# Second attention of a four-layer kernel: another instruction order on each engine, the second normalization on ScalarE, and the weights of two attentions asked for a stage earlier

## The reference

```python
def fake_quant(x, s, qn, qp):                       # round to a step of s, clipped
    xc = jnp.clip(x / s, qn, qp)
    xr = xc + jax.lax.stop_gradient(jnp.round(xc) - xc)
    return s * xr
qkv = jnp.einsum('bnc,dc->bnd', x, Wqkv)...         # x: normed tokens
q = fake_quant(q, s_q, -4, 3) * scale
k = fake_quant(k, s_k, -4, 3)
v = fake_quant(v, s_v, -4, 3)
attn = jnp.einsum('bhnd,bhmd->bhnm', q, k)
attn = fake_quant(attn / N, s_attn, 0, 7)
out = jnp.einsum('bhnm,bhmd->bhnd', attn, v)
out = fake_quant(out, s_after, -4, 3)
return out @ Wproj.T + bproj
```

## Time and profile before

| what | value |
|---|---|
| time, median of 3 runs | 2672.78 us |
| the profiled execution's own time | 2677.54 us |
| its span | 2675.4 us, 52026 instructions |
| granted TensorE clock, mean | 0.907 of full speed |
| PE busy | 2346.2 us, 88% |
| DVE busy | 1339.4 us, 50% |
| ACT busy | 852.6 us, 32% |
| POOL busy | 493.8 us, 18% |
| second attention | 615.6 to 876.8 us of the span |
| third attention, start | 1253.2 us |

### The profile page before, as it was taken

The page is one execution under the profiler, slowest core; times in us unless marked ns, Lnnn a source line. Parts: engine busy times, 40 slices in busy tenths (PEclk is TensorE's granted clock), DMA queues, the critical chain, the costliest instruction groups (busy, mean ns, idle before and its releaser), DMA issues. The chain is left out here.

```text
span 2675.4 us, 52026 instructions
## 1 busy us (share of the span) xinstructions
PE 2346.2 (88%) x17821; PEld 2039.7 (76%) x17821; DVE 1339.4 (50%) x3887; ACT 852.6 (32%) x2082; POOL 493.8 (18%) x583
## 2 busy tenths in 40 slices
PE   6968999995998489997999766999978899999997
PEld 5967999993666389986788655778747788888886
DVE  1665333333786711112688743555566446372744
ACT  0421222222555033332232212343444343343421
POOL 0214322221332334443122101000011000010100
PEclk8978999995787699998999856999989999999999
DMA  4103545512110267673000001000000452726355
GB/s 105 26 23 113 180 139 169 178 46 54 33 34 16 81 198 243 213 228 104 18 18 9 1 1 28 8 7 9 7 12 26 142 146 66 205 54 174 90 150 156
DMA packets 241583, 234.74 MB, mean 88 GB/s; under 512 B 29624, under 2 KB 223022, under 8 KB 241326
## 3 DMA queue, kind: packets, MB, share of 16 engines
q1 hardware_dynamic: 226798, 203.52, 26.8%
q0 software_dynamic: 11520, 27.54, 3.1%
q10 hardware_dynamic: 3136, 2.03, 0.3%
HBM read 277.77 MB, written 35.45 MB: 117 GB/s over the span
## 5 line engine op out<-in xcount | busy, mean ns | idle before, releaser
L740 PE MATMUL f_pg<-f_vxT,f_w 128*128 128x128 f32 x2112 | 261.2, 278 | 3.0 <-DVE f_vxT L810 3.0
L740 PEld LDWEIGHTS f_pg<-f_vxT,f_w 128*128 128x128 f32 x2112 | 251.8, 194 | 7.9 <-DVE f_vxT L810 4.4
L752 PE MATMUL f_po<-f_wd,f_hid 128*128 128x192 f32 x1440 | 254.3, 326 | 1.2 <-DVE f_vout L836 0.7
L752 PEld LDWEIGHTS f_po<-f_wd,f_hid 128*128 128x128 f32 x1440 | 231.2, 190 | 2.0 <-issue 1.7
L713 POOL DMA_INDIRECT f_answers<-f_vout,f_to_row x120 | 118.5, 987 | 418.6 <-DVE f_vout L834 250.7
L821 DVE TENSOR_TENSOR f_hid<-f_silu,f_pg 128x128 f32<-128x128 f32 x336 | 81.5, 283 | 218.8 <-ACT f_silu L789 204.0
L789 ACT ACTIVATE f_silu<-f_pg 128x128 f32<-128x128 f32 x336 | 78.2, 276 | 292.9 <-PE f_pg L746 275.2
L794 ACT ACTIVATE f_hid<-f_pg,f_b 128x128 f32<-128x128 f32 x384 | 111.2, 368 | 186.8 <-issue 102.2
L810 DVE COPY f_vxT<-f_pt 128x256 f32<-128x256 f32 x120 | 50.5, 421 | 208.5 <-PE f_pt L732 208.5
L746 PE MATMUL f_pg<-f_vxT,f_wr 64*128 64x128 f32 x2112 | 150.9, 284 | 0.0
L1900 DVE TENSOR_REDUCE a_low<-a_s_bank 96x6 f32<-96x1152 f32 x64 | 86.7, 1354 | 116.5 <-PE a_s_bank L1755 116.1
(11 more groups left out here) (396 smaller groups left out, 4807.2 us busy)
## 6 DMA issues: line engine op xcount, KB each, us to landing
f_wd<-in_L_ffn_W SPq DMA_DIRECT2D x64, 576.0 KB
f_wd<-in_L_ffn_WdT SPq DMA_DIRECT2D x56, 576.0 KB
f_w<-in_L_ffn_W SPq DMA_DIRECT2D x64, 384.0 KB
f_w<-in_L_ffn_WgT SPq DMA_DIRECT2D x56, 384.0 KB
f_w<-in_L_ffn_WuT SPq DMA_DIRECT2D x56, 384.0 KB
s_w<-in_w SPq DMA_DIRECT2D x64, 288.0 KB, 3.7
f_wr<-in_L_ffn_W SPq DMA_DIRECT2D x128, 96.0 KB
s_w<-in_w SPq DMA_DIRECT2D x64, 192.0 KB, 4.1
```

The source lines that it names most:

```text
L740: pe.matmul(pg[j][:, a * ROWS:(a + 1) * ROWS], lift[a][r][:, j * 128:j * 128 + 128], xT[r][:, 0, :], start=(a == 0), stop=False, skip_grou ...
L752: last = pe.matmul(po[:, 0:D], hid[r][:, j, :], wd[r][:, j, :], start=(at == 0), stop=(at == FC - 1))
```

## The change

Three things. (1) `SecondWeights` and `ThirdWeights` are made before `tokens_of_places` of the mixture before, and ACT issues their DMAs there (17 and 7), from its own queue; both attentions only wait for them. The five small DVE instructions that work out scale factors stand at the start of the second attention. (2) The second normed rows (`norm_out`) are written by ACT, as two activations with a scale and a bias each; DVE makes the bias (-mean times the inverse root) in `shift_of`. (3) PE, ACT and DVE have another order in their loops; `route_scores` and the copy of its logits come one iteration later. The loop of POOL is as before, but for the name of the semaphore it waits for ahead of it.

```diff
@@ tokens_of_places
         def _(act):
+            begin_early(act)
             act.wait_ge(used, PAIRS_OF)
@@ moe
         route(k, name, logits, wts, place_of, expert_of, fresh, E, ROWS, probs_first=b2 is not None)
+        next_weights = early(ctx)
...
-            tokens_of_places(k, name, place_of, from_row, to_row, slots, weights.begin)
+            tokens_of_places(k, name, place_of, from_row, to_row, slots, weights.begin, next_weights.begin)
...
-        after(answers, wts)
+        after(next_weights, answers, wts)
+class SecondWeights:
...
+    def begin(self, act):
+        wqk_src, wv_src, wproj_src, bias_src, steps_src, routerT = self.sources
+        act.dma_start(self.padded[:], halves(wqk_src)).then_inc(self.loaded, 16)
+        act.dma_start(self.wv[:], halves(wv_src)).then_inc(self.loaded, 16)
+        act.dma_start(self.router[:], halves(routerT)).then_inc(self.loaded, 16)
+        act.dma_start(self.s[:], steps_src.broadcast_to([H2, 5])).then_inc(self.loaded, 16)
+        act.dma_start(self.bias[:], bias_src.broadcast_to([H2, D])).then_inc(self.loaded, 16)
+        by_head_rows = wproj_src.rearrange("(h r) n -> h r n", r=32)
+        for head in range(HEADS):
+            e, at_row = divmod(head * DH, H2)
+            act.dma_start(self.wp[at_row:at_row + DH, e, :], by_head_rows[head, 0:DH]).then_inc(self.loaded, 16)
@@ attention1, SyncE
-            bring(0)
-            sp.dma_start(padded[:], halves(wqk_src)).then_inc(S["loaded"], 16)
...
+            for m in range(6):
+                bring(m)
@@ attention1, TensorE
-            for n in range(B + 2):
+            for n in range(B + 3):
                 if n < B:
                     scores(n, 0)
+                if n >= 3:
+                    route_scores(n - 3)
+                if n + 1 < B:
+                    turn_in(n + 1)
                 if 1 <= n <= B:
                     weigh(n - 1, 1)
                 if n < B:
                     scores(n, 1)
                 if n + 1 < B:
-                    turn_in(n + 1)
+                    queries(n + 1)
                 if n < B:
                     scores(n, 2)
-                if n + 1 < B:
-                    queries(n + 1)
                 if 1 <= n <= B:
                     project_out(n - 1)
                 if n < B:
                     scores(n, 3)
-                    weigh(n, 0)
                 if n + 1 < B:
                     keys(n + 1)
                 if n < B:
+                    weigh(n, 0)
                     scores(n, 4)
-                if n >= 2:
+                if 2 <= n <= B + 1:
                     turn_normed(n - 2)
                 if n + 1 < B:
                     values(n + 1)
                 if n < B:
                     scores(n, 5)
-                if n >= 2:
-                    route_scores(n - 2)
@@ attention1, ScalarE
+            def norm_out(n):
+                act.wait_ge(S["shift"], n + 1)
+                if n >= KEPT:
+                    act.wait_ge(kept[n % KEPT], 32 * (n // KEPT))
+                    act.wait_ge(S["grown"], n - KEPT + 1)
+                for t in range(2):
+                    last = nc.scalar.activation(rows2[n % KEPT][:, t, :], h[:, 2 * n + t, :], ACT.Identity,
+                                                scale=root[1][:, t, :], bias=shift[n % 2][:, t, :])
+                last.then_inc(S["rows2"], 1)
...
                     keep_scores(n, 0)
+                if n + 1 < B:
+                    copy(xT, t_bank, "turned", n + 2, "xT")
                 if 1 <= n <= B:
                     keep_o(n - 1)
...
                     keep_scores(n, 5)
+                if 1 <= n <= B:
+                    norm_out(n - 1)
@@ attention1, VectorE
+            def shift_of(n):
+                dve.wait_ge(S["root1"], n + 1)
+                nc.vector.scalar_tensor_tensor(out=shift[n % 2][:], in0=mv[1][:, :, 0:1], scalar=-1.0, in1=root[1][:],
+                                               op0=ALU.mult, op1=ALU.mult).then_inc(S["shift"], 1)
...
+                if n >= 3:
+                    keep_logits(n - 3)
...
+                if ahead:
+                    take_q(n + 1)
                 if front:
                     take_scores(n, 2)
-                if ahead:
-                    take_q(n + 1)
+                if second:
+                    spread_in(n + 2)
                 if front:
                     take_scores(n, 3)
                 if back:
                     add(n - 1)
                 if ahead:
                     take_k(n + 1)
+                if front:
+                    take_scores(n, 4)
                 if back:
                     dve.wait_ge(S["added"], n)
                     spread_of(1, n - 1)
-                if front:
-                    take_scores(n, 4)
                 if second:
-                    spread_in(n + 2)
+                    norm_in(n + 2)
                 if ahead:
                     take_v(n + 1)
                 if front:
                     take_scores(n, 5)
                 if back:
-                    norm_out(n - 1)
-                if n >= 2:
-                    keep_logits(n - 2)
-                if second:
-                    norm_in(n + 2)
+                    shift_of(n - 1)
```

More of the change, by code:

```diff
@@ L1188, in _, with __init__, attention1 @@
                     highest(n)
-def attention1(k, wqk_src, wv_src, wproj_src, bias_src, steps_src, answers, wts, routerT, logits, normed, E):
+class SecondWeights:
+    def __init__(self, k, ctx, sources, E):
+        self.sources = sources
+        self.padded = k.sb("a1_padded", [H2, 2, 2 * PAD], ctx=ctx)
+        self.wv, self.wp = k.sb("a1_wv", [H2, 2, D], ctx=ctx), k.sb("a1_wp", [H2, 2, D], ctx=ctx)
+        self.bias, self.router = k.sb("a1_bias", [H2, D], ctx=ctx), k.sb("a1_router", [H2, 2, E], ctx=ctx)
+        self.s = k.sb("a1_s", [H2, 5], ctx=ctx)
+        self.loaded, self.LOADED = k.sem("a1_loaded"), 16 * 17
+    def begin(self, act):
[9 more added lines that the diff above has]
+            act.dma_start(self.wp[at_row:at_row + DH, e, :], by_head_rows[head, 0:DH]).then_inc(self.loaded, 16)
+def attention1(k, weights, answers, wts, logits, normed, E):
     nc, h, stats = k.nc, k.h, k.stats
@@ L1220, in attention1 @@
         mv, var, root = ([one(f"{x}{r}", [H2, 2, n]) for r in range(2)] for x, n in (("mv", 2), ("var", 1), ("root", 1)))
-        half = one("half", [H2, 2, 1])
+        half, shift = one("half", [H2, 2, 1]), ring(2, "shift", [H2, 2, 1])
         p_bank, o_bank, t_bank, b_bank = (k.ps(f"a1_{x}_bank", [128, 512], ctx) for x in ("p", "o", "t", "b"))
@@ L1224, in attention1 @@
         S = {x: k.sem(f"a1_{x}") for x in (
-            "loaded", "preset", "packed", "consts", "step", "collected", "var0", "var1", "root0", "root1", "rows", "biased", "turned",
+            "shift", "preset", "packed", "consts", "step", "collected", "var0", "var1", "root0", "root1", "rows", "biased", "turned",
             "xT", "q_in", "q8", "q", "k_in", "k8", "k", "v_in", "v8", "v", "scores", "at8", "at", "weighed", "o8", "o",
@@ L1454, in keep_o @@
                 nc.scalar.activation(o8[:], view(o_bank), ACT.Identity, scale=fac[:, 3:4]).then_inc(S["o8"], 1)
[L1456 to L1462, removed]
+            def norm_out(n):
[7 more added lines that the diff above has]
+                last.then_inc(S["rows2"], 1)
+            act.wait_ge(weights.loaded, weights.LOADED)
             for d in range(2):
@@ L1948, with __init__, begin, attention2 @@
 PAIRS = HEADS // 2
-def attention2(k, wqkv_src, feat_src, halves_src, wproj_src, bias_src, gamma_src, beta_src, answers, wts):
+class ThirdWeights:
+    def __init__(self, k, ctx, sources):
+        self.sources = sources
+        self.w, self.wp = k.sb("a2_w", [H2, 2, 3 * D], ctx=ctx), k.sb("a2_wp", [H2, 2, D], ctx=ctx)
+        self.bias, self.gamma, self.beta = (k.sb(f"a2_{x}", [H2, D], ctx=ctx) for x in ("bias", "gamma", "beta"))
+        self.feat = k.sb("a2_feat", [128, HALF_HEADS * FEATURES], ctx=ctx)
+        self.minus_half = k.sb("a2_minus_half", [H2, 32], ctx=ctx)
+        self.loaded, self.LOADED = k.sem("a2_loaded"), 16 * 7
+    def begin(self, act):
+        wqkv_src, feat_src, wproj_src, bias_src, halves_src, gamma_src, beta_src = self.sources
+        act.dma_start(self.w[:], halves(wqkv_src)).then_inc(self.loaded, 16)
+        act.dma_start(self.feat[:], feat_src).then_inc(self.loaded, 16)
+        act.dma_start(self.wp[:], halves(wproj_src)).then_inc(self.loaded, 16)
+        act.dma_start(self.bias[:], bias_src.broadcast_to([H2, D])).then_inc(self.loaded, 16)
+        act.dma_start(self.minus_half[:], halves_src).then_inc(self.loaded, 16)
+        act.dma_start(self.gamma[:], gamma_src.broadcast_to([H2, D])).then_inc(self.loaded, 16)
+        act.dma_start(self.beta[:], beta_src.broadcast_to([H2, D])).then_inc(self.loaded, 16)
+def attention2(k, weights, answers, wts):
     nc, h, stats = k.nc, k.h, k.stats
@@ L2001, in bring @@
```

(8 more changed lines are left out.)

73 lines of the change are left out of this document (26 added, 47 removed).

## The result

The changed kernel took 2728.74 us (median of 4 runs, 2721.35 to 2732.55) against 2672.55 for the kernel before on the same chip (2671.81 to 2676.34): a ratio of 1.0199, 95% interval 1.0179 to 1.0219. It is slower by 56.2 us, where +48.1 was forecast: 2728.7 lies in the whole range and in the likeliest case's own one, 7.8 us above the forecast.

A forecast was written before the change was run, and what follows sets the result against it. PE, busy 88% of the span, was taken as the bound, with its clock deciding. Loop +56.0, loop end +0.5, starts -5.6 and -2.8 gave +48.1 us on 2672.78: 2720.9, range 2668 to 2732 (likeliest case's own 2704 to 2732).

The forecast's parts named there:

- likeliest case: Second attention's loop: scores between f32 pieces keep PE at 1.2 GHz; loop +56.0 us, kernel 2720.9 us, chance 0.62.
- The first three blocks: Start of the second attention's loop, taken as already at the low clock before: 48.2 us less 0.5.
- A block: Second attention's loop: each of the other twelve blocks is PE bound at 1.2 GHz and takes 18.4 us.
- The stalls nearly vanish: Loop block at 1.2 GHz: the 7.9 us chain to queries is nearly covered by PE's own work.
- the stand of DVE: DVE in each loop block: norm_in waits about 1.7 us for POOL to make two roots.
- the shift: shift_of on DVE, the small instruction gained for ACT's second norm: 0.17 us, priced like L1533.
- twice 3.5: PE's own work up to weigh in a block: 3.5 us at full clock, some 7.0 at 1.2 GHz.
- The starts: Early weights let PE begin sooner: -5.6 us in the second attention, -2.8 in the third.
- DMAs in the placing stages: Weight DMAs issued by ACT in the placing stages fit its idle time and cover: cost 0.
- Loop end and behind: End of the second attention's loop: a shift, a slower norm and a later logit copy, +0.5 us.
- clock holds, faster: Rival: filled thin part keeps the loop at 2.4 GHz, blocks 13.0 to 13.5 us, kernel 2653.9 us; chance 0.18.
- clock comes back in each block: Rival: the clock returns later in each loop block, 15.2 us a block, kernel 2682.5 us; chance 0.12.

The follow-up runs named there:

- e1: Kernel before, with scores(n, 2) moved on PE from ahead of queries to between queries and project_out: 2750.87 us, ratio 1.0254.
- e3: Changed kernel, with scores(n, 2) put ahead of queries on PE, so that queries and project_out touch again: 2700.60 us, ratio 1.0086.
- e9: Changed kernel, plus eight filler matmuls (f32, result not read) just ahead of queries on PE: 2704.05 us, ratio 1.0068.
- e5: Changed kernel, with both edits of e2 and e3 (POOL's roots exchanged, score rounds 1 and 2 together): 2695.49 us, ratio 1.0062.
- e4: Kernel before, with only the early weights of the change, loops as before: 2666.28 us, ratio 0.9954.
- e2: Changed kernel, with POOL's two roots exchanged so that norm_in no longer waits for the second variance: 2722.98 us, ratio 1.0156.
- e6: e5 plus eight filler matmuls (f32, result not read) just ahead of queries on PE: 2695.88 us, ratio 1.0062.
- e7: e6 with ACT's two norm activations moved from the end of their block to behind keep_scores(n, 1) of the next: 2669.95 us, ratio 0.9963.
- e10: e7 with the filler in two places, six matmuls ahead of weigh and six ahead of queries: 2638.84 us, ratio 0.9836.
- e12: e10 with four and four filler matmuls instead of six and six, and from block 0: 2636.57 us, ratio 0.9838.
- e11: e8 with the filler from block 0 instead of block 1: 2640.83 us, ratio 0.9839.
- e8: e4 plus filler matmuls from block 1, five ahead of weigh and four ahead of queries: 2647.42 us, ratio 0.9880.

## Why the prediction was right, and where it was mis-sized

*The clock* (likeliest case): right. 0.50 through the loop, as said, from 652.6; the forecast had it low from 640. The reason given, scores between the f32 pieces, is borne out by e1 (cause put into the kernel before: clock gone), e3 (taken out of the changed one: clock back in part) and e9 (a long f32 stretch put in elsewhere: clock back in part). The rule of the Trainium skill weighed there ("TensorE: Matmul & The Clock Gate", section "What's actually happening": activity releases the throttle) is not borne out if activity means a busy PE: 94% busy over 233 us stayed at 1.2 GHz. What it is in the scores that does not count (bf16, 32 partitions, their size) stays open, since no run varied one alone, and so does why the same adjacent pieces bring the clock back in some blocks and not in others (e5).

*The first three blocks*: mis-sized, 47.7 forecast and 39.3 measured, -8.4. I took the clock to be low from the start, and read it so in the kernel before, which is not quite right. In both kernels it rises as `queries`, `keys` and `values` of block 0 run close together (here 623.60 to 632.44, with waits of 0.57 and 0.73 us); before, it fell again after 3.4 us, and now after 20.5. It is the order of the loops that makes it stand, not the early weights: e4, with these alone, loses it after 3.4 us too, and every run with the new loops (e2, e3, e5, e6, e7, e9, e10, e12) keeps it for 20 us or more. Which part of the order does it was not tried alone; in the old order filler in block 0 makes it stand too (e11).

*A block*: mis-sized, 18.4 forecast and 19.30 measured, twelve times 0.9 or +10.8. "The stalls nearly vanish" is the step that failed: 1.12 us of idle time are left ahead of `queries`, where the sum had almost none. The sum set a chain of 7.9 us, from the end of `scores 4` to `queries`, against 8.3 us of PE's own work in it. Measured are 8.6 and 7.5, and the difference is the 1.12 us. Both terms were off:

- The chain: the stand of DVE was right (1.54 us, forecast 1.7, bounds 1.5 to 1.8, 18.5 us in twelve blocks). But the shift was priced at 0.17 us by a one-input neighbour and took 0.97, and that is the whole excess. ACT's norms took 0.99 us, the upper bound, where 0.75 was forecast; they take as long in e2, where PE waits 0.18 us.
- PE's work: "twice 3.5" us up to `weigh` was 6.2 (803.49 to 809.67). Not every piece takes twice its time at 1.2 GHz: `values` goes from 1.47 to 2.77, a round of scores from 0.36 to 0.55.

PE's list without idle time, 18.18 us, is close to the 18.31 of the forecast. e2, without the stand and the long shift, has blocks of 18.36, which the forecast had said for a kernel with the stand.

*The starts*: -6.2 for -5.6, and -4.0 for -2.8, beyond the bound of 3.4 (rows of the third were ready sooner than I allowed). *DMAs in the placing stages*: 0 was right: in the second of them `f_before` to the start of `f_tp_summed` takes 21.3 us in both kernels, and from there to `f_tp_turned` 20.2 where it was 20.9; in the first this is 20.7 where it was 20.2. *Loop end and behind*: +0.5 forecast, +5.3 measured (1.9 + 3.4), mostly outside the change. Measured less forecast: -8.4, +10.8, -0.6, -1.2 and +4.8, and two stretches that had no term, -1.1 ahead of the stage and +0.2 before the first `a_v`: +4.5, which takes 48.1 to the 52.5 of the span (0.1 is rounding). The other 3.7 of the 56.2 is that the profiled execution of before stood 5.0 above its median in this comparison (2672.55) and that of after only 1.2 above its own. That the forecast came within 8 us is in part luck: the first three blocks and the other twelve were off in opposite directions, each by more than the total.

The rival "clock holds, faster" did not occur, but it had a truth: its conditions (a filled thin part, POOL's order put right) are e10's and e12's, and these are 1.6% faster than before. The rival "clock comes back in each block" (15.2 a block) has nearly the block of e7 (15.0), but e7 has filler and three orders mended, so the nearness says nothing for its sum.

## What to carry to other kernels

Before reordering a PE list, look at the granted clock and at which pieces stand together where it rises: at 1.2 GHz the f32 pieces here take nearly twice their time, and one small piece moved between two of them cost 2.5% of this kernel (e1). If the clock comes and goes, matmuls of no use placed in the idle gaps can pay (1.6% here, e10 to e12); in one place only, they cost what they gave (e6). Then follow the order of the small engines (POOL's two roots here) as carefully as that of the big one, and price a small instruction by one with the same number of inputs, beside what runs at that time.

## What the runs showed of the hardware that was not expected

A DVE instruction of two SBUF inputs and two columns took 0.97 us beside a POOL addition, and 0.15 us (median 149 ns, e2) when it ran apart from it. POOL's own `add_bias` took 1.54 us beside DVE and 0.99 in e2, right behind the root. Both ended at 809.86 us. What made POOL's longer was not told apart: `take_v` and `take_scores 5` ran beside it as well. The Trainium skill, "SBUF — State Buffer", section "Who interferes with whom", says that a DVE instruction with two inputs in SBUF contends with a GpSimd instruction that reads SBUF; the traces agree, with 0.82 us as the price of one such meeting here.

Extra work made a loop faster: 18 more PE instructions in a block took it from 13.4 to 14.0 us down to 12.21 (e4 to e8), as all of PE's pieces then ran at 2.4 GHz. A held clock did not always make the times steadier: the ten runs of e4 lie 28.8 us apart, the four of e8 7.5 and the six of e11 6.0, but the six runs each of e10 and e12, with the clock up as well, 20.2 and 20.4. What differs there stays open.
